# Second routed expert stage: five weight places instead of four, each asked for five chunks ahead

## What is computed

```
res = x                                   # after the latent attention, 2 x 1024 x 256
t = rmsnorm(x, g2)                        # 2048 tokens
probs = softmax(t @ router_w)             # 8 experts
vals, idx = top_k(probs, 2)
w = vals / sum(vals);  gate = sum(one_hot(idx) * w)
hid = silu(t @ w1[e]) * (t @ w3[e])       # 256 -> 512, for each expert e
y = sum over e of gate[e] * (hid @ w2[e]) # 512 -> 256
out = res + y
```

## Time and profile before

| | us |
|---|---|
| median of 3 runs | 3037.45 |
| lowest, highest | 3037.12, 3042.05 |
| the profiled execution | 3032.85 |
| its span (first to last instruction) | 3031.6 |
| PE busy | 2913.8 (96% of the span) |
| POOL busy | 884.8 (29%) |
| second routed stage, from the first product of chunk 0 to the end | 2789.36 to 3031.6 |

### The profile page before, as it was taken

The page is one execution under the profiler, slowest core; times in us unless marked ns, Lnnn a source line. Parts: engine busy times, 40 slices in busy tenths (PEclk is TensorE's granted clock), DMA queues, the critical chain, the costliest instruction groups (busy, mean ns, idle before and its releaser), DMA issues.

```text
span 3031.6 us, 46800 instructions
## 1 busy us (share of the span) xinstructions
PE 2913.8 (96%) x17974; PEld 2225.7 (73%) x17974; DVE 2089.5 (69%) x3874; ACT 1203.2 (40%) x2262; POOL 884.8 (29%) x1341
## 2 busy tenths in 40 slices
PE   7999999999999999999999999999999989998998
PEld 5778777667766776677689999866797754456988
DVE  6996788568856885687377888795225867777422
ACT  5443333552355326532223333352113635665221
POOL 2207401100110010001146565561252432111665
PEclk8999999999999999999999999999999998999999
DMA  6100100020002000200022222102382011114765
GB/s 180 38 1 1 31 28 1 15 65 8 1 14 73 1 1 14 72 0 1 1 79 79 88 77 84 48 3 77 113 297 64 1 42 50 36 33 159 231 188 119
DMA packets 108440, 182.94 MB, mean 60 GB/s; under 512 B 29130, under 2 KB 80236, under 8 KB 102716
## 3 DMA queue, kind: packets, MB, share of 16 engines
q1 hardware_dynamic: 89596, 99.16, 10.6%
q0 software_dynamic: 18624, 80.80, 8.6%
HBM read 193.86 MB, written 18.90 MB: 70 GB/s over the span
## 4 chain that ended last, share of the span: by engine, by line
PE 75%; DVE 14%; DMA 3%; issue 3%; ACT 3%; POOL 1%; SPq 0%; DVEq 0%; POOLq 0%; ACTq 0%
PE psum L485 9%; PE psum L507 8%; PE psum L1581 7%; PE psum L1593 7%; PE psum L2059 5%; PE psum L2831 5%; PE psum L2014 5%; DMA out<-shared,Vt 2%; PE psum L1289 2%; PE psum L2844 2%; PE psum L477 2%; PE psum L861 2%; PE psum L3508 2%; PE psum L2982 2%; PE psum L3528 1%
## 5 line engine op out<-in xcount | busy, mean ns | idle before, releaser
L485 PE MATMUL psum<-Vt,shared 128*128 128x256 f32 x1600 | 358.9, 379 | 0.2
L507 PE MATMUL psum<-Kt,xnTt 128*128 128x512 f32 (+1 forms) x960 | 346.4, 511 | 0.3 <-ACT xnTt L601 0.3
L485 PEld LDWEIGHTS psum<-Vt,shared 128*128 128x128 f32 x1600 | 297.7, 190 | 38.2 <-issue 1.0
L507 PEld LDWEIGHTS psum<-Kt,xnTt 128*128 128x128 f32 x960 | 179.9, 191 | 161.6 <-issue 158.0
L249 POOL TENSOR_SCALAR root_v<-meanvar 128x8 f32<-128x8 f32 (+2 forms) x18 | 8.4, 465 | 860.7 <-DVE meanvar L227 860.7
L1593 PEld LDWEIGHTS psum<-expert_w,prep 128*128 128x128 f32 x1024 | 194.6, 190 | 77.7 <-issue 57.4
L1593 PE MATMUL psum<-expert_w,prep 128*128 128x256 f32 x1024 | 240.8, 379 | 0.0
L1581 PE MATMUL psum<-weights,expert_w 128*128 128x512 f32 x512 | 240.3, 593 | 0.0
L1507 DVE SCALAR_TENSOR_TENSOR bias<-Kt,small,bias 128x1232 f32<-128x1232 f32 x96 | 149.2, 1554 | 129.4 <-ACT Kt L1491 128.4
L3837 DVE CUSTOM_DVE_ANT_0 psum<-psum,expert_w 128x128 f32<-128x128 f32 (+7 forms) x256 | 191.3, 777 | 61.9 <-PE psum L3508 57.5
L3706 ACT ACTIVATE prep<-psum 128x512 f32<-128x512 f32 (+3 forms) x384 | 163.6, 501 | 60.0 <-PE psum L3531 58.0
(11 more groups left out here) (602 smaller groups left out, 6575.3 us busy)
## 6 DMA issues: line engine op xcount, KB each, us to landing
weights<-in_L_ffn_w SPq DMA_DIRECT2D x32, 512.0 KB, 4.6
expert_w<-in_L_ffn_w SPq DMA_DIRECT2D x32, 512.0 KB, 4.3
expert_w<-in_L_xattn_Wf SPq DMA_DIRECT2D x16, 512.0 KB, 6.1
weights<-q_parts SPq DMA_DIRECT2D x31, 144.0 KB
weights<-k_parts SPq DMA_DIRECT2D x93, 48.0 KB
weights<-in_L_xattn_Wk SPq DMA_DIRECT2D x4, 1024.0 KB, 5.0
weights<-in_L_xattn_Wv SPq DMA_DIRECT2D x4, 1024.0 KB, 7.9
weights<-in_L_xattn_Wq SPq DMA_DIRECT2D x4, 1024.0 KB, 5.7
```

Of the source, the lines that this page charges most:

```text
L485: ins = pe.matmul(o_bank(t), wide_probT[:, t % 2, c, :], Vt[:, t // TB, c, :], start=(c == 8), stop=(c == 7))
L507: ins = pe.matmul(flat[:, par * 3 * BANK + at:par * 3 * BANK + at + cols], xnTt[:, par, k, :], Kt[:, t // TB, k, src:src + cols], start=(k ...
```

## The change

The second routed stage gets a fifth place for weights, the upper half of `expert_w`. `WSLOTS` becomes a pair, (4, 5), by stage. In the second stage chunk c uses place c % 5; round i fetches the weights of chunk i+5 instead of i+4, into the place that chunk i has left; before the loop the weights of chunk 4 are fetched too, once POOL has taken the last values of the latent attention from `expert_w`. The comparison for skipped fetches is with the chunk five before in the second stage, for both of its lists. The rows still have four places and are fetched four chunks ahead. `counts_made` and `tokens_found` become one semaphore, with the counts that are waited for renumbered; the number of semaphores stays the same (one more for the fifth place).

```
-    chosen_w_landed = [sem(f"chosen{n}_landed") for n in range(4)]
+    chosen_w_landed = [sem(f"chosen{n}_landed") for n in range(5)]
...
-    WSLOTS, RSLOTS = 4, 4
+    WSLOTS, RSLOTS = (4, 5), 4
...
-    slots_of = (slots4, (expert_w[:, 0:3072], flat_V1[:, 0:3072], weights[:, 0:3072], weights[:, 3072:6144]))
+    slots_of = (slots4, (expert_w[:, 0:3072], flat_V1[:, 0:3072], weights[:, 0:3072], weights[:, 3072:6144], expert_w[:, 3072:6144]))
...
+    def weights_before(r, s, n):
+
+        return sum(len(range(s, TOTALS[q], WSLOTS[q])) for q in range(r) if s < WSLOTS[q]) + len(range(s, n, WSLOTS[r]))
...
     def act_counts(act, q):
-        act.wait_ge(counts_made, 2 * q + 2)
+        act.wait_ge(counts_or_tokens_made, 3 * q + 2)
...
-        total = FOUND[q]
+        total, turns = FOUND[q], WSLOTS[min(q, 1)]
...
-        then(dve, dve.tensor_tensor(same[:, WSLOTS:], expert_of[:, WSLOTS:], expert_of[:, 0:total - WSLOTS], ALU.is_equal))
+        then(dve, dve.tensor_tensor(same[:, turns:], expert_of[:, turns:], expert_of[:, 0:total - turns], ALU.is_equal))
...
-        dve.wait_ge(tokens_found, q + 1)
+        dve.wait_ge(counts_or_tokens_made, 3 * q + 4)
...
-            pool.indirect_dma_start(slots_of[r][c % WSLOTS], None, experts, bass.IndirectOffsetOnAxis(w_row[:, c:c + 1], 0),
-                                    bounds_check=E * P - 1, oob_is_err=False).then_inc(chosen_w_landed[c % WSLOTS], 16)
+            pool.indirect_dma_start(slots_of[r][c % WSLOTS[r]], None, experts, bass.IndirectOffsetOnAxis(w_row[:, c:c + 1], 0),
+                                    bounds_check=E * P - 1, oob_is_err=False).then_inc(chosen_w_landed[c % WSLOTS[r]], 16)
...
         fetch_weights(3)
+        if r == 1:
+            pool.wait_ge(values_taken, HEADS)
+            fetch_weights(4)
...
-            if c + WSLOTS < total:
+            if c + WSLOTS[r] < total:
                 pool.wait_ge(routed_second, base + c + 1)
-                fetch_weights(c + WSLOTS)
+                fetch_weights(c + WSLOTS[r])
...
         def first(c):
-            w = slots_of[r][c % WSLOTS]
-            pe.wait_ge(chosen_w_landed[c % WSLOTS], 16 * uses_before(r, c % WSLOTS, c + 1, WSLOTS))
+            w = slots_of[r][c % WSLOTS[r]]
+            pe.wait_ge(chosen_w_landed[c % WSLOTS[r]], 16 * weights_before(r, c % WSLOTS[r], c + 1))
```

More of the change, by code:

```diff
@@ L198, in build @@
         sem(n) for n in ("narrow_zeroed", "narrow_made", "narrow_kept", "narrow_spread", "values_made", "values_kept"))
-    places_made, codes_scaled, hot_made, tokens_found, tokens_made = (
-        sem(n) for n in ("places_made", "codes_scaled", "hot_made", "tokens_found", "tokens_made"))
-    counts_made, counts_kept = sem("counts_made"), sem("counts_kept")
+    places_made, codes_scaled, hot_made, tokens_made = (
+        sem(n) for n in ("places_made", "codes_scaled", "hot_made", "tokens_made"))
+    counts_or_tokens_made, counts_kept = sem("counts_or_tokens_made"), sem("counts_kept")
     rows_ready, rows_turned, rows_kept = sem("rows_ready"), sem("rows_turned"), sem("rows_kept")
@@ L2512, in pe_tables @@
         pe.matmul(psum[:, 6, 0:P], ones[:, :], earlier, start=True, stop=True)
-        pe.matmul(psum[:, 6, P:P + 1], earlier, ones[:, 0:1], start=True, stop=True).then_inc(counts_made, 1)
+        pe.matmul(psum[:, 6, P:P + 1], earlier, ones[:, 0:1], start=True, stop=True).then_inc(counts_or_tokens_made, 1)
     def dve_tables(dve):
-        dve.wait_ge(counts_made, 1)
+        dve.wait_ge(counts_or_tokens_made, 1)
         then(dve, dve.tensor_copy(iota, psum[:, 6, 0:P]))
@@ L2551, in pe_tile_counts @@
         pe.matmul(counts_bank(q)[:, 2 * P:3 * P], both.rearrange("p t e -> p (t e)"), ones[:, :],
-                  start=True, stop=True).then_inc(counts_made, 1)
+                  start=True, stop=True).then_inc(counts_or_tokens_made, 1)
     def pe_counts(pe, q, both):
@@ L2557, in pe_counts @@
         pe.matmul(counts_bank(q)[:, 0:P], tile_counts(q), earlier_tiles, start=False, stop=True)
-        pe.matmul(counts_bank(q)[:, P:P + E], tile_counts(q), of_expert, start=True, stop=True).then_inc(counts_made, 1)
+        pe.matmul(counts_bank(q)[:, P:P + E], tile_counts(q), of_expert, start=True, stop=True).then_inc(counts_or_tokens_made, 1)
     def act_counts(act, q):
-        act.wait_ge(counts_made, 2 * q + 2)
+        act.wait_ge(counts_or_tokens_made, 3 * q + 2)
         act.copy(tile_counts(q), counts_bank(q)[:, 2 * P:3 * P]).then_inc(counts_kept, 1)
@@ L2603, in dve_places @@
         passed = srow(856, total * (E - 1), q).rearrange("p (c e) -> p c e", e=E - 1)
-        dve.wait_ge(counts_made, 2 * q + 3)
+        dve.wait_ge(counts_or_tokens_made, 3 * q + 3)
         of_all = counts(q)[1]
@@ L2617, in dve_places @@
         then(dve, dve.tensor_reduce(expert_of, passed, AX.X, ALU.add))
-        then(dve, dve.tensor_tensor(same[:, WSLOTS:], expert_of[:, WSLOTS:], expert_of[:, 0:total - WSLOTS], ALU.is_equal))
+        then(dve, dve.tensor_tensor(same[:, turns:], expert_of[:, turns:], expert_of[:, 0:total - turns], ALU.is_equal))
         then(dve, dve.tensor_scalar(expert_row, expert_of, float(P), partition, ALU.mult, ALU.add))
-        then(dve, dve.scalar_tensor_tensor(expert_row[:, WSLOTS:], same[:, WSLOTS:], float(4 * E * P), expert_row[:, WSLOTS:],
+        then(dve, dve.scalar_tensor_tensor(expert_row[:, turns:], same[:, turns:], float(4 * E * P), expert_row[:, turns:],
                                            ALU.mult, ALU.add))
@@ L2690, in pe_tokens @@
                             start=(j == 0), stop=(j == J - 1))
-        ins.then_inc(tokens_found, 1)
+        ins.then_inc(counts_or_tokens_made, 1)
     def dve_tokens(dve, q):
```

## The result

| | before | after |
|---|---|---|
| median of 20 runs each, us | 3037.61 | 3047.33 |
| lowest and highest | 3031.78, 3044.61 | 3040.39, 3053.72 |
| span of the profiled execution | 3031.6 | 3046.7 |
| first product of chunk 0 | 2789.36 | 2792.76 |
| the stage, from there to the end | 242.2 | 253.9 |

What follows compares the result with a forecast made beforehand. POOL and DMA, not PE, were taken to set the time from chunk 10 to 31. Extra fetches cost +4.3 us, earlier issue wins 2.7: +1.6, so 3039.0 us on the median, range 3033.0 to 3043.5.

Steps and rivals of the forecast that it cites:

- Round 3: POOL's round 3 now fetches chunk 8's weights: cost taken as 0.6 us, from 0 (absorbed) to 1.97 (in full).
- Rounds 14 and 23: POOL rounds that now fetch weights: 1.85 us each, 3.7 us for the two, bounds 3.4 and 3.9.
- Sum for POOL: Cost of the four extra fetches on POOL's rounds from 27 on: +4.3 us, bounds 3.4 and 5.9.
- The win on PE: Earlier weights let PE start chunk 32's first product 2.7 us sooner (1.1 to 4.5), limited by rows landing later.
- The shift stays to the end: After chunk 32 all fetches are skipped and rounds are shorter than PE's steps, so the net +1.6 us lasts.
- Chunk 4's fetch ahead of the loop: Its 1.3 us of issue hide in POOL's 8.03 us idle time before the loop: cost 0.
- the renumbered semaphore: Merged semaphore with renumbered counts: no instruction more, same order on PE, cost 0.
- the bytes: Queue q0 moves 52.7 MB in the stage, with 27 weights fetches that move something instead of 23.
- The signs named for the profile: PE's waits before chunk 17 under 2 us in all, some later on transposes; fetch rounds near 6.4; chunks 9-38 170-175 us.
- rival 3: Extra fetches in the dense stretch cost their full transfer, 5.3 us each: +13.2 us, 3050.6; chance 0.11.
- Rival 1: Weights supply becomes sufficient, so all 11.3 us of PE's waits go: 3026.2; chance 0.07.
- Rival 2: Rows do not hold PE back; weights decide: +4.3 - 5.6 = -1.3 us, 3036.1; chance 0.22.

Runs made afterwards that it cites:

- x_nostore: Changed kernel without the late store of the gates; the first half's gates are stored ahead twice, so some gates are wrong; 1.0028 of the kernel before.
- x_late8: Changed kernel with chunk 8's weights fetch moved from POOL's round 3 to round 4, all data and transfers kept; 1.0010 of the kernel before.
- x_no8: Changed kernel with the transfer of chunk 8's weights in round 3 left out, that chunk computed with other weights; 1.0008 of the kernel before.
- x_no3late: Changed kernel with the weights transfers of chunks 17, 24 and 32 left out, these computed with other weights; 1.0003 of the kernel before.
- x_all: Changed kernel with rows asked for five chunks ahead, chunk 8's weights fetched in round 4 and the store of the gates split in two; 1.0008 of before.
- x_rows5: Changed kernel with a fifth place for rows too, asked for five chunks ahead from round 5 on; 1.0018 of the kernel before.
- y_fetch7: Kernel before the change, four places, with one more real transfer: chunk 7's weights in round 3, same data; 1.0022 of the kernel before.
- x_gates: Changed kernel with the store of the gates in two parts, the first half's gates stored before the stage; 1.0021 of the kernel before.

## Why the prediction was wrong

- **The failed step is "Round 3": "From 0 (absorbed) to 1.97 (in full); I take 0.6, since scatter 3 goes out only behind this fetch, but has time."** It had no time: result 3 landed late enough to hold result 4 for 5.83 us. And the step asked only what stood behind the fetch on q0. SP's store of the gates was issued 2.3 us later in the same trace, on a queue that the prediction never read, and the rows of chunk 9 can't be fetched before it has landed. Measured: 7.7 us at round 5, 8.2 at round 27, 6.7 in time. Even the upper bound was 4 times too small, as it was the price of a fetch where no store stands in POOL's way; without the store, the runs have 3.1 (x_nostore) and 3.3 us (x_late8) for it.
- **Rounds 14 and 23: right.** Forecast 1.85 us each, measured 2.05 (x_no8), 2.15 (after, from 7.7 to 12.0), 2.25 (x_no3late).
- **Sum for POOL.** Forecast +4.3 at round 27, measured +12.0. The difference, 7.7, is 7.1 of round 3 and 0.6 of the two others.
- **The win on PE: the right mechanism, a size at the low end.** Rows, not weights, released every wait from chunk 9 on. Forecast 2.7 us over the rounds' lag (1.1 to 4.5), measured 1.3. With rows five ahead it would have been 4.5.
- **Its worth: wrong.** "The shift stays to the end" held for PE, but the end hangs on POOL's chain of results. It was in near balance with PE before, and what PE wins over POOL doesn't shorten the stage. By the trace +10.7 on PE became +11.7 at the end, and -1.1 in x_all became +2.8.
- **Chunk 4's fetch ahead of the loop, the renumbered semaphore, the bytes: right.** Rounds 0 to 4 start within 0.2 us of before, and q0 moved 52.74 MB for 52.7 forecast.
- **The signs named for the profile.** That PE's waits "before chunk 17 shrink to under 2 us in all" was wrong: those for chunks 9 and 10 alone are 2.73 and 2.53. From chunk 9 to chunk 38 PE takes 179.2 us (2851.86 to 3031.10), for 170 to 175. Rounds 6 to 12 take 6.79 us each, for about 6.4 (44.59 us before, and the lag grows from 5.9 to 8.8), just under the 6.8 named as the limit to rival 3. The waits on L2825 with the rows as releaser came.
- **Rivals.** Rival 3 had the sign and not the place: no extra fetch costs its full transfer in the dense part (2.0 to 2.25 us each, for its 5.3). Rival 1 did not happen, and x_rows5 shows that a supply without the limit of rows would not have brought it either. Rival 2 fell by the fourteen waits for rows.

For the store, the runs show 4.9 us with no weights in front, 14.7 and 15.0 with, and 12.7 with half the packets. The Trainium skill, page "DMA: Bandwidth & Descriptors", section "Queues, rings and completion order", says that each DMA engine takes turns between the queues for which it has work, a packet at a time. By that rule SP's store has a share of each engine beside the gather on q0, but must take turns with it for as long as the gather lasts. The trace does not show such a share at first: from 2831 to 2836 q0 has 1.43 MB moved and q1 9 packets of 2064. The 726 packets that run after 2838 beside the next weights agree with it in the direction. The rule's size can't be checked here: what the profile counts as a packet has 8 bytes, and a packet of that page of the Trainium skill holds several descriptors. And 12.7 us with half the packets says that their number is the smaller part. Whether the engines had not taken up the store in its first 4.7 us, or SP's queue had not handed it over, no run shows.

The same page of the Trainium skill, section "Anatomy of one DMA — SWDGE (gpsimd) path", would give a result of 131 KB 2.0 + 0.3 = 2.3 us, as an estimate. The rows at the end, with DMA otherwise idle, show a next result 4.4 to 4.6 us later, and the chain of waits 3.66 to 3.93 us for its DMA. The trace does not agree; by the Trainium skill's figure, as an estimate, these rounds would be some 1.5 us shorter.

## What to carry to other kernels

An extra transfer is not priced by its bytes in the average round: lay it into the trace at the moment where it will start, and list every transfer of every queue that is in flight in the 15 us behind it, and who waits for each. A small transfer on another engine's queue can be the one that decides, above all when it is made of many tiny packets and the next phase can't begin without it (here its share, 4.6 of 7.7 us, is shown by traces and not by the times). And before crediting a win on the busiest engine, follow the last work of the kernel to its end: if another engine's chain arrives within a few us of it, the win ends there.

## What was not expected of the hardware

- A store of 16 KB in 8-byte packets on SP's queue landed in 4.9 us with no large gather ahead (x_no8), in 14.4 to 15.0 us with one of 1.573 MB issued 2.3 us ahead of it and another 3.2 us behind (after, y_fetch7, x_rows5), and in 12.7 us with half the packets (x_gates). While the first of the two gathers moved, 9 of its 2064 packets ran (after).
- The same accumulating scatter of 131 KB held the next one back for 2.9 to 3.1 us at the end of the kernel, where DMA has nothing else, and for 4.7 to 6.4 us just behind one or two sets of weights.
- In 4 of the 14 profiled executions the granted clock dropped to its lower level for some 7 us near the start of the stage (a mean of 0.77 over its first 15 us, for 1.00), and made everything after it 3.3 us later. In the 30 us before, PE was busy for the same 25.1 us at a mean clock of 0.94, in x_no8 as in after, which kept 1.00. Two single traces compared without regard to this would have given the first four chunks a cost that they don't have.
